# First gather layer: one PSUM bank for each of a block's four table chunks, one bank for its sums, and the second layer's relation weights added up on VectorE beside the first table

## What is computed

```python
for l in range(2):
    W = jnp.einsum('rb,bio->rio', coeffs[l], bases[l])      # 8 matrices 256x256
    h = jnp.einsum('ni,rio->rno', x, W)                     # the "table"
    msg = h[edge_type, src] * deg_inv[dst][:, None]
    agg = jax.ops.segment_sum(msg, dst, num_segments=num_nodes)
    x_new = agg + x @ self_loops[l]
    if l < 1:
        x_new = jax.nn.relu(x_new)
    x = x_new
```

## Time and profile before

| | us |
|---|---|
| median of three runs (3622.14 to 3641.18) | 3629.47 |
| the profiled execution's own time | 3602.8 |
| its span, first to last instruction | 3601.1 |

### The profile page before, as it was taken

One profiled execution on the slowest core, in us unless ns is written; L12 is line 12 of the kernel. 1 busy time (PEld: TensorE's weight loads), 2 busy tenths in 40 slices (PEclk: granted clock), 3 DMA queues, 4 the chain that ended last, 5 costly groups with the idle time before them and its releaser, 6 DMA issues. The chain is left out here.

```text
span 3601.1 us, 37652 instructions
## 1 busy us (share of the span) xinstructions
PE 2442.1 (68%) x9592; PEld 1750.2 (49%) x9592; DVE 924.5 (26%) x2885; ACT 657.0 (18%) x1423; POOL 1648.2 (46%) x1712
## 2 busy tenths in 40 slices
PE   6999356667666667766669166666766666657197
PEld 3777234445444445444446154544545445445065
DVE  2120112222222222222223032332323323224233
ACT  4455111111111111111112001111112111110033
POOL 0000554455444554444540655555655556652534
PEclk9999778888888888888889577777777878778577
DMA  8655533333333333333331323333332333321441
GB/s 221 223 222 190 163 105 110 111 105 115 109 106 105 105 117 107 111 110 106 114 111 73 110 84 89 88 90 87 89 92 85 91 91 89 92 82 45 130 128 53
DMA packets 155518, 401.32 MB, mean 111 GB/s; under 512 B 35102, under 2 KB 86657, under 8 KB 140348
## 3 DMA queue, kind: packets, MB, share of 16 engines
q0 software_dynamic: 81648, 219.65, 21.0%
q10 hardware_dynamic: 36156, 126.22, 9.1%
q1 hardware_dynamic: 37585, 53.92, 5.5%
HBM read 262.69 MB, written 141.04 MB: 112 GB/s over the span
## 5 line engine op out<-in xcount | busy, mean ns | idle before, releaser
L487 POOL DMA_INDIRECT gnn_ring<-table,g_idx x1564 | 1511.8, 967 | 1604.7 <-PE gnn_pagg L530 840.0
L530 PE MATMUL gnn_pagg<-gnn_ring,gnn_oh 128*128 x3904 | 1125.3, 432 | 387.4 <-issue 337.2
L530 PEld LDWEIGHTS gnn_pagg<-gnn_ring,gnn_oh 128*128 128x128 f32 x3904 | 779.5, 213 | 723.0 <-issue 615.3
L514 DVE TENSOR_TENSOR gnn_oh<-gnn_col,g_dst 128x256 f32<-128x256 f32 x976 | 408.0, 425 | 1510.9 <-DVEq L49 1344.8
L711 PE MATMUL gnn_pm<-gnn_whigh,gnn_high 128*128 128x512 f32 x392 | 209.0, 533 | 369.2 <-ACT gnn_rows L762 269.1
L711 PEld LDWEIGHTS gnn_pm<-gnn_whigh,gnn_high 128*128 128x128 f32 x392 | 98.7, 252 | 422.1 <-ACT gnn_rows L762 291.0
L1014 ACT ACTIVATE gnn_qe<-gnn_pq,gnn_bq 128x128 f32<-128x128 f32 x98 | 36.0, 367 | 1062.9 <-remote 1019.0
L711 PE MATMUL gnn_pm<-gnn_wlow,gnn_high 128*128 128x512 f32 x392 | 195.2, 498 | 0.0
L711 PE MATMUL gnn_pm<-gnn_whigh,gnn_low 128*128 128x512 f32 x392 | 194.7, 497 | 0.0
L762 ACT COPY gnn_rows<-gnn_pm 128x512 f32<-128x512 f32 x196 | 110.7, 587 | 449.4 <-DMA pre_bs<-in_L_gnn_bases 257.1
L366 PE MATMUL pre_psum<-pre_whigh,pre_high 128*128 128x512 f32 x392 | 159.4, 407 | 10.6 <-DVE pre_low L294 7.0
(11 more groups left out here) (172 smaller groups left out, 2320.0 us busy)
## 6 DMA issues: line engine op xcount, KB each, us to landing
table<-pre_rows ACTq DMA_DIRECT2D x49, 1024.0 KB, 3.9
table<-gnn_rows ACTq DMA_DIRECT2D x48, 1024.0 KB
gnn_ring<-table,g_idx POOLq DMA_INDIRECT x1564
pre_bs<-in_L_gnn_bases SPq DMA_DIRECT2D x64, 240.0 KB
bucket<-gnn_zrow SPq DMA_DIRECT2D x16, 650.0 KB
g_xT<-bucket SPq DMA_DIRECT2D x20, 520.0 KB, 6.3
x1T<-gnn_x1T ACTq DMA_DIRECT2D x49, 128.0 KB
gnn_x1T<-x1T ACTq DMA_DIRECT2D x49, 128.0 KB
```

The lines of the kernel that those rows point to most:

```text
L487: eng.indirect_dma_start(self.ring[:, q % RG, t, 0:D], None, self.g.table[self.l][:, :], bass.IndirectOffsetOnAxis(ap=self.g.idx[:, at:at ...
L514: self.nc.vector.tensor_tensor(self.oh[:, h, :, :], self.col[:, :].unsqueeze(1).to_broadcast([P, n, P]), self.g.dst[:, ds(q * TPG + h * n, ...
L530: mm = nc.tensor.matmul(pagg[:, k, 0:self.width], self.oh[:, h, i, :], self.ring[:, ds(q & (RG - 1), 1), t, 0:self.width].rearrange("p o n ...
```

## The change

- `gnn_first`: `pm` has four banks, one per chunk; `multiply` no longer waits for copies between chunks. `pagg` has one bank in this layer. The transposition's output shares the fourth chunk's bank, so `turn(b)` waits until ScalarE has copied block b-1's chunks (`rows_ok`).
- Second layer's W: the eight pieces on TensorE and ScalarE, their trip through DRAM and the load at the start of `gnn_first` are gone. Instead SyncE loads each of the 30 bases (256 KB) whole during startup, and VectorE adds them up in fp32, 240 multiply-adds of 128x512 (`terms`), into `second_wr`, which outlives startup. Between low parts it does 7 of them per block as a rule, 1 where there are statistics, 3 where there is normalisation, 0 at blocks 0 and 14.
- The split of W into high and low for this layer: ScalarE's two casts come at once; VectorE's two subtractions move behind block 0's step, and TensorE waits for them at block 1, not ahead of block 0. `second_wr` then serves as the buffer for ScalarE's copies.

The core of the diff:

```diff
 def startup
-            if n % WB < 2 or n >= NPC:
+            if n % WB < 2:
+        def terms_beside(b):
+            return 0 if b in (0, 2 * G) else 1 if chunk_at(b) else 3 if chunk_at(b - 1) else 7
+        first_terms = [min(NBASE * R, sum(terms_beside(c) for c in range(b))) for b in range(NB + 1)]
 sync
-                if b % EVERY == 2 and b // EVERY < NPC:
-                    load(NPC + b // EVERY)
+                if b == 0:
+                    eng.dma_start(cr[:, :], a["coeff_rows"]....to_broadcast([P, NBASE * R])).then_inc(cr_in, 16)
+                for n in range(NBASE):
+                    if base_at[n] == b:
+                        if n >= AT_ONCE:
+                            eng.wait_ge(added, n - AT_ONCE + 1)
+                        eng.dma_start(base[:, n % AT_ONCE, :, :], a["L0_gnn_bases"][1][n]....).then_inc(base_in[n % AT_ONCE], 16)
 vector
+            def terms(lo, hi):
+                for i in range(lo, hi):
+                    n, r = divmod(i, R)
+                    if r == 0:
+                        eng.wait_ge(base_in[n % AT_ONCE], 16 * (n // AT_ONCE + 1))
+                        ...
+                    w = wr[:, :, r * D:(r + 1) * D]
+                    if n:
+                        ins = V.scalar_tensor_tensor(out=w, in0=base[:, n % AT_ONCE, :, :], scalar=cr[:, i:i + 1], in1=w,
+                                                     op0=ALU.mult, op1=ALU.add)
+                    else:
+                        ins = V.tensor_scalar(w, base[:, 0, :, :], cr[:, i:i + 1], None, ALU.mult)
+                    if r == R - 1:
+                        ins.then_inc(added, 1)
 tensor, scalar
-                if piece_after(b) is not None:
-                    weights(piece_after(b))
 class Aggregate
-        self.pagg = s.ps("pagg", [P, 2, 512])
+        self.pagg = s.ps("pagg", [P, 1 + l, 512])
 def gnn_first
-        rows = s.sb("rows", [P, 2, R * D])
+        rows = wr
-        pm = s.ps("pm", [P, W, 512])
+        pm = s.ps("pm", [P, NC, 512])
-        pT = s.ps("pT", [P, 512])
+        pT = pm[:, NC - 1, 0:D]
-            load_weights(eng, g, rows, 1, wr_in)
 vector
-            for h in range(H2):
-                eng.wait_ge(split_ok, h + 1)
-                ins = V.tensor_tensor(wlow[:, h, :], rows[:, h, :], whigh[:, h, :], ALU.subtract)
             for b in range(NB):
                 step(b, b % 2)
+                if b == 0:
+                    for h in range(H2):
+                        eng.wait_ge(split_ok, h + 1)
+                        ins = V.tensor_tensor(wlow[:, h, :], wr[:, h, :], whigh[:, h, :], ALU.subtract)
 tensor
-                for n in range(2 * W):
-                    reach(eng, chunk_free)
+                for n in range(NC):
-            def turn():
+            def turn(b):
                 reach(eng, xn_ok)
+                if b:
+                    eng.wait_ge(rows_ok, b)
-            eng.wait_ge(split_ok, H2 + 1)
```

More of the change, by code:

```diff
@@ L332, in _ @@
                     edges()
+                terms(first_terms[b], first_terms[b + 1])
+            eng.wait_ge(added, NBASE)
         @block.tensor
@@ L443, in _ @@
                 eng.wait_ge(stored[k], 16 * ((NB + 1 - k) // 2))
-            for k in range(WB):
-                eng.wait_ge(w_out[k], 16 * (NPC // WB + (NPC // 2 if k < 2 else 0)))
 class Aggregate:
@@ L788, in _ @@
                 eng.sem_inc(kept[k], 16)
[L789 removed]
             for h in range(H2):
[L791 removed]
+                nc.scalar.copy(whigh[:, h, :], wr[:, h, :]).then_inc(split_ok, 1)
             own_part()
@@ L1268, in program @@
         had = nc.snapshot_sems()
-        startup(nc, g, a)
-        nc.clear_and_free_semaphores(nc.allocated_since(had))
-        nc.all_engine_barrier()
-        gnn_first(nc, g, a)
+        with nc.sbuf_tensor("second_wr", [P, H2, R * D], F32) as wr:
+            startup(nc, g, a, wr)
+            nc.clear_and_free_semaphores(nc.allocated_since(had))
+            nc.all_engine_barrier()
+            gnn_first(nc, g, a, wr)
         r = Routed(Scope(nc, ctx, "rt"))
```

120 lines of the change are left out of this document (62 added, 58 removed).

## The result

The changed kernel took 3448.66 us (median of 4 runs, 3436.11 to 3464.78) where the kernel before took 3625.8 us (4 runs, 3619.0 to 3641.18): ratio 0.951, 95% interval 0.945 to 0.957, so 177 us faster. Forecast were 272 us. For these first runs and profiles the record names no chip.

What follows compares the result with a forecast made beforehand. A loop of waits, with TensorE's signals told late after GpSimd's gather bursts, was taken to bound the first gather layer. Banks 243 plus startup 29.4 gave 272 us off 3629.5: 3357 us, range 3240 to 3510 (about 0.8).

Steps and rivals of the forecast that it cites:

- The bound and its four terms: First gather layer: GpSimd's wait per block is 2.74 + 0.64 + 4.75 + 3.64 = 11.77 us, from late-told TensorE signals.
- rival 5: First gather layer: banks have no effect, only startup gains; 3600 us, 0.8% faster; chance 0.04.
- Banks: First gather layer: without the copy wait, 5.39 us leave each of 45 GpSimd waits; gain taken as 243 us.
- the sum behind them is first in line as GpSimd stops: First gather layer: all 24 chunk matmuls are out by burst's end, leaving 6.4 us from burst to burst.
- Rival 1: First gather layer: chunks must still run after the burst; gain there only 29 to 117 us, 3571 to 3483; chance 0.16.
- rival 3: First gather layer: bursts merge because the lag is never made up; 55 us more per such block, slower; chance 0.08.
- turn's wait for `rows_ok`: nothing: First gather layer: turn's wait for the previous block's copies stands behind a sum of over ten us; costs nothing.
- Start of the layer: First block of the first gather layer: subtractions fall inside the first burst; nothing more counted, bounds -5 to +4.5 us.
- Startup, 29.4 us: Startup, bound by TensorE: eight weight pieces of 3.68 us each go; VectorE's 240 terms fit its idle time.
- rival 4: Startup: VectorE becomes the bound, banks' gain intact; up to 93 us back, 3450 us; chance 0.04.
- Second layer, unchanged: Second gather layer, whose code is the same: forecast change 0 us.
- Adding the difference to the median: Whole kernel: the median's 26.7 us above the profiled 3602.8 us is kept, so 272 us come off 3629.5.

Runs made afterwards that it cites:

- banks_late: Kernel before with only the four chunk banks, one sum bank and shared transposition bank, on chip 12: 3437.28 us, ratio 0.957.
- lock_late: Changed kernel plus a TensorE wait before each sum until its last chunk matmul is told, on chip 12: 3558.75 us, ratio 0.991 to the kernel before.
- banks_only: Kernel before with only the four chunk banks, one sum bank and shared transposition bank, on chip 11: 2610.66 us, ratio 1.000.
- subs_early: Changed kernel with VectorE's two subtractions of the second layer's weights back ahead of block 0, on chip 2: 3427.36 us, no ratio given.
- hold: Changed kernel with subtractions ahead of block 0, next block's one-hots ahead of keys and held until the first chunk is told, chip 13: 3498.81 us, ratio 0.964.
- again_late: Changed kernel once more, unchanged, on chip 13: 3451.19 us, ratio 0.953 to the kernel before.

## Why the prediction was right in its shape and off in its size

- *The bound and its four terms.* Right for chips with late signals, and there near in size: the ordinary block shown waits 6.65 us against 6.4, all 36 wait 7.4 on average and last 26.44 us for 26.66. What fills the wait was only partly right. The four copies come in one piece 2.9 us behind the burst, as forecast, but the sum was not put out before the burst ended in 31 of 36 cases, and in the block shown the one-hots, which were said to be there, ended its wait. On chip 12, with the banks alone, ordinary blocks take 25.1 us and more of them are long, so the near hit of 26.66 belongs to one profile. That the chip had late signals at all was luck: the prediction has no case in which they are prompt, and on chip 11 the change is worth 1.0%, near rival 5's share but for another reason.
- *"Banks", 243 us.* This is the term that was mis-sized. In the 43 blocks it is 142.8 us for 231.8. Of the 89 missing, the six new long blocks make 238.9 - 6 x 26.4 = 80.5, and block 40, which gained nothing, 6.9 (44.6 for 43.1 - 5.4). The step at fault is "the sum behind them is first in line as GpSimd stops", applied to every block. In the kernel before, with the wait for copies, none of 41 sums began inside a burst and no block but 40 was long; without it some transpositions come so late in a burst that they are told behind it. banks_late shows that this comes with the banks (159 us in all there). That the wait had kept TensorE in step with the bursts is my reading of it; lock_late, which puts a wait back, still has four long blocks beside 40.
- *Rival 1, rival 3.* Both live in the long blocks: in block 12 the chunks' copies come one by one at 814.11, 816.61, 818.24 and 819.60 us (2.50 us apart at the clock of 0.50, then 1.63 and 1.36), rival 1's sign, and the trigger is rival 3's, a signal that is not made up within the burst. Rival 3's price was 55 us a block, measured are some 13, and a long block is followed by an ordinary one.
- *"turn's wait for `rows_ok`: nothing", "one bank for sums: nothing".* Right as far as shown: in the ordinary block L747 starts at 1152.74, just behind VectorE's last step (1152.37 + 0.32), when the chunks' copies have been over for 13 us, and banks_only on chip 11 is at 1.000.
- *Start of the layer, nothing (-5 to +4.5) beside the first wait's 5.4.* +10.9. Block 0's chunks waited for the two subtractions, in the timeline:

```profile
462.56 4.49 DVE L696 TENSOR_TENSOR gnn_wlow<-second_wr,gnn_whigh 128x2048 fp32r<-128x2048 f32 x2
...
467.11 0.80 PE L738 MATMUL gnn_pm<-gnn_whigh,gnn_high 128*128 128x512 f32 x1 [25.97 <-DVE gnn_wlow L696]
```

  "Inside that burst" was wrong: they stand behind the keys, those behind the own part, and that was told 10.3 us after the burst (449.49 to 459.79). Moving them (subs_early) shortened the first block and lengthened the second; 3 us were left.
- *Startup, 29.4 us.* 26.0, and 25.5 on chip 11. TensorE's work shrank by 29.5 us, as forecast; 3.5 us came back as idle time, for the low parts (8.9 us in six waits, where it was 7.0 in one) and for a copy of ScalarE's (5.5 for 3.6), which is rival 4's sign at a small size. The terms were priced well: 232 of them keep VectorE busy for 159.4 us, 0.69 each. One by itself lasts 0.747, so neighbours overlap.
- *Second layer, unchanged.* +26.4 in the first pair of profiles. Its 43 blocks take 1141.9 to 1147.5 us in the five traces of chips 2 and 12, with or without the weights' part, and 1171.3 and 1175.1 in those of hold and again_late on chip 13. That goes with the chip and not with the change. The first two profiles have 1147.1 and 1169.6 us, so they look like two chips, but the record can't tell. If they are two, the first layer's 142.8 us hold some of that difference, too; banks_late, at 143.8 us beside an equal second layer, speaks for the size all the same.
- *Adding the difference to the median.* Two profiles 143 us apart stood for medians 177 apart. The deduction from one profile carries that error, too.

What stays open: why TensorE's signals are late on chips 2, 12, 13 and the first one and prompt on 11, and what decides whether a sum's end is told 3 or 5 to 10 us late at the same age of a burst. A lower clock of TensorE goes with the long blocks (0.69 for 0.44 us at L747), but after long waits it would be there as a result as well.

## What to carry to other kernels

Before a wait is removed, ask what else it holds in step: here, as I read the runs, the wait for copies kept a block's later signals inside the right part of a burst, and a third of the forecast gain went to the few blocks that were long without it. Measure on more than one chip before a mechanism is called the hardware's: the same change was worth 4.9% on one and 1.0% on another, and it took runs of the parts on both kinds to tell whether the gain was the banks' or the weights'. And a wait put on an engine's own queue costs its run-ahead, 2.3 us a block here even where nothing is late.

## What the runs showed of the hardware that I had not expected

- The same kernel takes 2611 us on chip 11 and 3590 to 3630 us on the others; the difference lies in the two gather layers (867 for 1207 to 1235 us, and 866 for 1170 to 1175, in 43 blocks of the changed kernel).
- On the slower chips TensorE's signals to VectorE and ScalarE come late while GpSimd issues indirect gathers (the end of a sum 3.1 us as a rule, up to 10 in long blocks of the changed kernel), and within 0.1 us while it issues as many direct transfers of the same bytes, or, on chip 11, even while it gathers.
- Two banks or four made no difference to the granted clock where signals were prompt: 1.00 in both.
